# Attention units multiplied in float32 without splitting, and PSUM copies moved from ScalarE to VectorE

## What is computed

```python
q = jnp.einsum('bsh,oh->bso', x, Wq)   # 16 heads of 32, rotated
k = jnp.einsum('bsh,oh->bso', x, Wk)   # 4 heads of 32, rotated
v = jnp.einsum('bsh,oh->bso', x, Wv)
scores = jnp.einsum('bhqd,bhkd->bhqk', q, k) * scaling
attn = jax.nn.softmax(scores, axis=-1)
out = jnp.einsum('bhqk,bhkd->bhqd', attn, v)
...
x = x + 0.5 * ffn(layernorm(x))
x = x + attention(layernorm(x))
x = x + 0.5 * ffn(layernorm(x))
```

## Time and profile before

| | us |
|---|---|
| median of 3 runs | 1826.81 (1823.87 to 1834.07) |
| profiled execution, whole | 1813.59 |
| its span, first to last instruction | 1811.8 |
| first to last exponential of the attention stage | 661.6 to 1226.1 |
| PE busy | 1685.2 (93%) |
| DVE busy | 1081.7 (60%) |
| ACT busy | 857.9 (47%) |
| POOL busy | 977.0 (54%) |

### The profile page before, as it was taken

The page is one execution under the profiler, slowest core; times in us unless marked ns, Lnnn a source line. Parts: engine busy times, 40 slices in busy tenths (PEclk is TensorE's granted clock), DMA queues, the critical chain, the costliest instruction groups (busy, mean ns, idle before and its releaser), DMA issues.

```text
span 1811.8 us, 25089 instructions
## 1 busy us (share of the span) xinstructions
PE 1685.2 (93%) x8596; PEld 1342.8 (74%) x8596; DVE 1081.7 (60%) x1846; ACT 857.9 (47%) x1274; POOL 977.0 (54%) x727
## 2 busy tenths in 40 slices
PE   6999999999977989999999999887799999999997
PEld 5888899898866756666666666545688889999885
DVE  4554322222587879999999999995445432222226
ACT  4322232222224358989898988872333122322220
POOL 3115673336522148989898989840030619550646
PEclk9999999999988989999999999998989999999998
DMA  9205543333640000000000000003010535432427
GB/s 341 87 25 217 207 175 131 120 132 114 192 140 1 1 2 1 1 1 1 1 1 2 1 1 2 12 13 142 1 52 1 223 121 194 161 140 85 166 83 243
DMA packets 54310, 160.01 MB, mean 88 GB/s; under 512 B 6704, under 2 KB 7600, under 8 KB 51632
## 3 DMA queue, kind: packets, MB, share of 16 engines
q1 hardware_dynamic: 41360, 84.74, 13.4%
q0 software_dynamic: 12832, 73.67, 11.5%
HBM read 102.29 MB, written 55.84 MB: 87 GB/s over the span
## 4 chain that ended last, share of the span: by engine, by line
PE 58%; DVE 18%; issue 8%; ACT 7%; DMA 7%; POOL 0%; SPq 0%; ACTq 0%; DVEq 0%; POOLq 0%
PE PS L1050 10%; PE PS L1052 9%; PE PS L1051 9%; DVE nmf L1831 5%; DVE Ph L1848 4%; PE PS L1246 4%; DMA xn<-x_routed 3%; ACT Ph L1526 3%; ACT PT L1519 2%; DMA xs<-x_routed 2%; PE PS L1279 2%; PE PS L1172 2%; PE PS L1280 2%; PE PS L1177 2%; PE PS L1175 2%
## 5 line engine op out<-in xcount | busy, mean ns | idle before, releaser
L1988 POOL TENSOR_TENSOR Pl<-PT,Ph 128x1024 fp32r<-128x1024 f32 x176 | 435.9, 2491 | 81.6 <-ACT Ph L1526 76.4
L1831 DVE TENSOR_REDUCE nmf<-PS 128x1 f32<-128x1024 f32 x256 | 307.7, 1213 | 29.0 <-PE PS L1246 26.7
L1519 ACT ACTIVATE PT<-PS 128x1024 f32<-128x1024 f32 x256 | 258.7, 1015 | 19.9 <-DVE Pl L1854 11.7
L1279 PE MATMUL PS<-Ph,V 128*65 128x512 f32 x512 | 206.5, 403 | 11.9 <-DVE Pl L1854 10.9
L1280 PE MATMUL PS<-Pl,V 128*65 128x512 f32 x512 | 201.9, 394 | 0.0
L1526 ACT ACTIVATE Ph<-PT 128x1024 fp32r<-128x1024 f32 x184 | 194.1, 1055 | 1.5
L1903 POOL TENSOR_TENSOR W<-raw,W 128x544 fp32r<-128x544 f32 x144 | 190.1, 1354 | 1.5
L1806 DVE TENSOR_TENSOR thid<-thid,PS 128x352 f32<-128x352 f32 x78 | 40.6, 521 | 245.8 <-ACT thid L1445 245.8
L1246 PE MATMUL PS<-KS,QS 96*128 96x512 f32 x512 | 170.8, 415 | 16.9 <-ACT PT L1519 11.3
L1264 PE MATMUL PS<-QS,KS 98*128 98x512 f32 x512 | 174.8, 423 | 6.0 <-DVE nmf L1831 5.8
L1445 ACT ACTIVATE thid<-PS 128x352 f32<-128x352 f32 x78 | 36.2, 464 | 260.4 <-PE PS L1177 260.4
(11 more groups left out here) (183 smaller groups left out, 4111.9 us busy)
## 6 DMA issues: line engine op xcount, KB each, us to landing
raw<-ffn_w POOLq DMA_DIRECT2D x18, 2176.0 KB, 10.3
y_routed<-ytile SPq DMA_DIRECT2D x78, 256.0 KB, 2.0
xn<-x_routed SPq DMA_DIRECT2D x40, 256.0 KB, 2.9
x_routed<-xq SPq DMA_DIRECT2D x1, 9984.0 KB, 28.7
xs<-x_routed SPq DMA_DIRECT2D x38, 256.0 KB, 3.6
raw<-ffn_w SPq DMA_DIRECT2D x6, 768.0 KB, 10.4
raw<-ffn_w SPq DMA_DIRECT2D x2, 2176.0 KB, 9.1
x_home<-X SPq DMA_DIRECT2D x4, 1024.0 KB, 5.7
```

The source lines that it names most:

```text
L1279: e.matmul(PS[0:VCOL, ob, :], V[:, b * QT + kt, g, :], high_part(u)[:, js], start=kt == 0, stop=False)
L1519: e.activation(PT[:, u % PTBUF, :], PS[:, i:i + 2, :].rearrange("p b n -> p (b n)"), ACT.Exp, scale=SCALE).then_inc(p_ready.sem, 1)
L1831: e.tensor_reduce(nmf[:, (n % 3) * REP + h, t:t + 1], PS[:, i:i + 2, :].rearrange("p b n -> p (b n)"), AX.X, ALU.max, negate=True).then_in ...
L1988: e.tensor_tensor(low_part(u)[:], PT[:, u % PTBUF, :], high_part(u)[:], ALU.subtract).then_inc(pl_pool.sem, 1)
```

## The change

- `in_full` names units that aren't split: in group 7 the last pair of each half head (u % 4 = 3), in the groups before one unit in sixteen (u % 16 = 11, also a last pair). Their values are two float32 matmuls that read PT itself and V as float32, three units after the scores (FULL_LAG) and behind the unit's other work on PE. The last pair is then done before pair 2, so pair 2 ends the half head (`ends_half`).
- `hi_on_vector` is now true in group 7 alone, for pair 1; in groups 0 to 6 ACT takes all high parts. `lo_on_vector`: pair 1 in group 7; pair 2 before, but not the one ahead of a float32 unit (u % 16 = 10), whose low part goes to POOL.
- The copy of the output bank to OT moves from ACT to DVE in all groups; that of the query stack to QS moves from ACT to DVE in groups 0 to 5 (`beside_heads`).
- A PT buffer that a float32 unit used is free when its values are done, not when its low part is.
- At the end, the last unit's float32 matmuls come ahead of the values of the unit before it.

```diff
-LAG = 5
+LAG, FULL_LAG = 5, 3
...
+def in_full(u):
+
+    return u % 4 == 3 if in_last_group(u) else u % 16 == 11
+
+
+def in_last_group(u):
+    return u // UNITS == len(KV_GROUPS) - 1
+
+
 def hi_on_vector(u):
-    return u % 4 == 1 or u // UNITS == len(KV_GROUPS) - 1 and u % 4 == 3
+    return in_last_group(u) and u % 4 == 1
 
 
 def lo_on_vector(u):
-    return u % 4 == 2 or u // UNITS == len(KV_GROUPS) - 1 and u % 4 != 0
+    return u % 4 == 1 if in_last_group(u) else u % 4 == 2 and u % 16 != 10
+
+
+def ends_half(u):
+
+    return in_full(u + 1) if u % 4 == 2 else u % 4 == 3 and not in_full(u)
...
-        w = in_flight[0] if in_flight[0] == u - LAG else None
+        w = u - LAG if u >= LAG and not in_full(u - LAG) else None
...
+        if u >= FULL_LAG and in_full(u - FULL_LAG):
+            work.append(("values", u - FULL_LAG))
...
+    for w in [v for v in range(end - LAG, end - 2) if not in_full(v)] + [end - 1, end - 2]:
         work.append(("values", w))
...
-                e.matmul(PS[0:VCOL, ob, :], V[:, b * QT + kt, g, :], high_part(u)[:, js], start=kt == 0, stop=False)
-                mm = e.matmul(PS[0:VCOL, ob, :], V[:, b * QT + kt, g, :], low_part(u)[:, js],
-                              start=False, stop=kt == QT - 1)
+                end = ends_half(u) and j == 1
+                if in_full(u):
+                    mm = e.matmul(PS[0:VCOL, ob, :], V[:, b * QT + kt, g, :].bitcast(F32), PT[:, u % PTBUF, js],
+                                  start=False, stop=end)
+                else:
+                    e.matmul(PS[0:VCOL, ob, :], V[:, b * QT + kt, g, :], high_part(u)[:, js],
+                             start=kt == 0, stop=False)
+                    mm = e.matmul(PS[0:VCOL, ob, :], V[:, b * QT + kt, g, :], low_part(u)[:, js],
+                                  start=False, stop=end)
...
-            elif kind == "turn":
+            elif kind == "turn" and not beside_heads(key[0]):
...
-                if u >= PTBUF:
-                    act.wait_ge(pl_dve if lo_on_vector(u - PTBUF) else pl_pool, u - PTBUF)
+                if u >= PTBUF and in_full(u - PTBUF):
+                    act.wait_ge(pv_done, u - PTBUF)
+                elif u >= PTBUF:
+                    parts_ready(act, u - PTBUF)
...
-                e.activation(OT[0:VCOL, :], PS[0:VCOL, out_bank(n, hf), :], ACT.Copy).then_inc(ot_ready.sem, 1)
...
+            elif kind in VALUES and is_whole(key) and ends_half(key[0]):
...
+                dve.wait_ge(pv_done, u)
+                if i >= 1:
+                    dve.wait_ge(ot_turned, *heads[i - 1])
+                e.tensor_copy(OT[0:VCOL, :], PS[0:VCOL, out_bank(n, hf), :]).then_inc(ot_ready.sem, 1)
+            elif kind == "turn" and beside_heads(key[0]):
+                n, t = key
+                dve.wait_ge(stack_turned, n, t)
+                e.tensor_copy(QS[n % 3][0:STK, :, t * P:(t + 1) * P],
+                              PS[0:STK, MISC, :].rearrange("p (h n) -> p h n", n=P)).then_inc(stack_ready.sem, 1)
```

More of the change, by code:

```diff
@@ L396, in order_of_work @@
     work.append(("heads_start",))
-    in_flight, outputs, maxima, lows = [], [], [], []
+    outputs, maxima, lows = [], [], []
     groups = len(KV_GROUPS)
@@ L404, in order_of_work @@
             work.append(("spare_bank",))
[L405 to L408, removed]
+        in_parts = u > 0 and not in_full(u - 1)
+        if in_parts:
+            work.append(("split_hi", u - 1))
+            if not lo_on_vector(u - 1):
+                work.append(("split_lo", u - 1))
         work.append(("scores", u))
-        in_flight.append(u)
         if lows:
             work.append(("place_low", *lows.pop(0)))
-        w = in_flight[0] if in_flight[0] == u - LAG else None
+        w = u - LAG if u >= LAG and not in_full(u - LAG) else None
         between = w is not None and unit(w)[3] > 0 and n + 1 < groups
@@ L424, in order_of_work @@
             maxima.append((n + 1, un // QT))
-        if len(in_flight) > 1 and lo_on_vector(in_flight[-2]):
-            work.append(("split_lo", in_flight[-2]))
+        if in_parts and lo_on_vector(u - 1):
+            work.append(("split_lo", u - 1))
         if w is not None:
-            in_flight.pop(0)
             work.append(("half_values", w, 1) if between else ("values", w))
-            if unit(w)[3] == QT // 2 - 1:
+            if ends_half(w):
                 outputs.append(unit(w)[:3])
+        if u >= FULL_LAG and in_full(u - FULL_LAG):
+            work.append(("values", u - FULL_LAG))
         if outputs and pair == 1:
@@ L440, in order_of_work @@
             work.append(("wo", un // QT))
-    work.append(("split_hi", in_flight[-1]))
-    work.append(("split_lo", in_flight[-1]))
-    for w in in_flight:
+    end = groups * UNITS
+    assert in_full(end - 1) and LAG > FULL_LAG
+    for w in [v for v in range(end - LAG, end - 2) if not in_full(v)] + [end - 1, end - 2]:
         work.append(("values", w))
-        if unit(w)[3] == QT // 2 - 1:
-            outputs.append(unit(w)[:3])
-        elif outputs and unit(w)[3] == 1:
+        if outputs:
             work.append(("store_head", *outputs.pop(0)))
+    outputs.append(unit(end - 2)[:3])
     work.append(("store_head", *outputs.pop(0)))
@@ L840, in macaron @@
             pv_done.plan(u)
-            if unit(u)[3] == QT // 2 - 1:
+            if ends_half(u):
                 ot_ready.plan(*unit(u)[:3])
@@ L899, in is_projected_after, with parts_ready @@
         return PROJECTED.index(t) >= n
+    def parts_ready(lane, u):
+        if in_full(u):
+            lane.wait_ge(p_ready, u)
+        else:
+            lane.wait_ge(pl_dve if lo_on_vector(u) else pl_pool, u)
     def high_part(u):
@@ L921, in macaron @@
     ends = [tuple(unit(key[0])[:3]) for kind, *key in work
-            if kind in VALUES and is_whole(key) and unit(key[0])[3] == QT // 2 - 1]
+            if kind in VALUES and is_whole(key) and ends_half(key[0])]
     end_place = {key: i for i, key in enumerate(ends)}
@@ L1842, in vector_program @@
                     dve.wait_ge(home_out[g])
+            elif kind in VALUES and is_whole(key) and ends_half(key[0]):
+                u = key[0]
+                n, h, hf, pair = unit(u)
+                i = end_place[n, h, hf]
+                dve.wait_ge(pv_done, u)
[7 more added lines that the diff above has]
+                              PS[0:STK, MISC, :].rearrange("p (h n) -> p h n", n=P)).then_inc(stack_ready.sem, 1)
             elif kind == "split_hi" and hi_on_vector(*key):
```

6 lines of the change are left out of this document (4 added, 2 removed).

## The result

The changed kernel takes 1861.52 us (median of 4 runs, 1855.08 to 1868.77) against 1827.0 for the kernel before beside it: a ratio of 1.0185, 95% interval 1.0128 to 1.0241. It is slower by 34 us, where the forecast was 1827 and the range ended at 1850. Its profiled execution has a span of 1864.9 us.

The account below looks back on a forecast made before the run. No engine's busy time was taken to bound the attention stage, but waits between engines. The terms +11.4 - 1.6 - 8.8 - 1.1 = 0 us, set on the median 1826.8, gave 1827 us; range 1807 to 1850.

Parts of the forecast that it names:

- groups 0 to 5: Attention stage, twelve periods of sixteen units (four half heads): each goes from 35.95 to 36.9 us, +11.4 us in all.
- last group: Last attention group, first to last exponential: PE becomes the bound, 51.4 us, -12.2; holds give back 3.4, so -8.8 us.
- Second half head: Second of a period's four half heads, groups 0 to 5: 8.48 us, with PE waiting 0.2 for the output copy.
- Rival 1: Attention stage: PE alone sets the pace, copies on DVE never late; period 33.8, 45 us faster, 1782; chance 0.12.
- Third: Third half head of a period, groups 0 to 5, no low part on DVE, maxima transposed: 8.46 us.
- First: First half head of a period (units 0 to 3), groups 0 to 5, DVE coming late after a float32 unit: 8.42 us.
- Fourth: Fourth half head of a period, groups 0 to 5, with the float32 matmuls in front of its last unit: 11.05 us.
- The 0.5 for a held low part: Added once per period in groups 0 to 5 for a DVE low part held by POOL's; estimate between 0 and 2.2.
- rival 4: PE's float32 matmuls: their passes don't overlap, 3.1 us a unit; +31 us, 1858; chance 0.07.
- rival 2: Attention stage: no holds occur and the float32 unit takes three passes; some 18 us faster, 1809; chance 0.11.
- The last group's holds: Last group: DVE's parts held behind POOL's low parts, output copy behind these; four times 0.85, 3.4 us lost.
- Rival 3: Attention groups: DVE's low part loses to POOL's and is held 2.2 us once a period; +20 us, 1847; chance 0.25.

## Why the prediction was wrong

| term of the sum | predicted | measured |
|---|---|---|
| groups 0 to 5 | +11.4 | +33.1 |
| group 6 | -1.6 | +4.4 |
| last group | -8.8 | -4.2 |
| tail behind the last exponential | -1.1 | -1.2 |
| sum | 0 | +32 |

(Measured: 1134.1 - 670.2 = 463.9 against 1092.4 - 661.6 = 430.8; then the stretches above against the earlier trace rows.)

**The step that failed** is the line of the Second half head, "maximum and output copy 1.84, PE's store 0.05 + 0.31, a unit 1.86": it lets PE run on to the store before it needs DVE's copy, and so finds a wait of 0.2. PE needs it one half unit sooner, 0.93, because the next half head's first values go into the same bank. The code shows it, `until_free(ob)` at pair 0, and the prediction used it for nothing. Rival 1's working has the same error, "PE asks for the copy at 2 x 1.86 = 3.7": the values ask at 2.8. With the deadline 0.93 earlier the wait is 0.2 + 0.93 = 1.13; the trace shows 1.16. The half head becomes 8.48 + 0.93, and 0.11 more because the copy reaches PE 0.82 after its start (874.09 to 874.91) and not 0.71: 9.52. Measured from low part to low part, 871.23 to 880.76, it is 9.53. From exponential to exponential the Third is 9.64, predicted 8.46, with the same wait of 1.16 (at 884.45); the First came out at 8.95 against 8.42, the Fourth at 10.69 against 11.05, and these two differences were not taken apart. The 0.5 for a held low part did not occur. Together, 1.05 + 1.18 + 0.53 - 0.36 - 0.5 = 1.9, the step from 36.9 to 38.80. Group 6 has the same single bank and the same error.

**Right** were the prices: the copy 0.60 to DVE's next (0.58), the low part 1.13 (872.36 - 871.23), the tail 5.71 against 5.75 (1268.01 to the end of the last row here). The float32 unit, in PE's timeline of the changed kernel with what follows it,

```profile
896.60 1.88 PE L1302 MATMUL PS<-PT,V 128*65 128x512 f32 x4
897.92 1.03 PE L1285 MATMUL PS<-QS,KS 98*128 98x512 f32 x2
898.79 0.39 PE L1305 MATMUL PS<-Ph,V 128*65 128x512 f32 x1
...
1273.32 0.40 PE L1307 MATMUL PS<-Pl,V 128*65 128x512 f32 x1
```

takes 898.79 - 896.60 less 0.46 for the scores, 1.73, where 1.74 was taken: rival 4 did not occur, and of rival 2 only the missing holds, in groups 0 to 6. (Its sum is a little off: 0.85 x 12, 3.4, 2.5 and 1 make 17 us, not 18.) Right too were PE's small wait for the store's last step, and DVE's idle time while a unit runs:

```profile
861.12 1.23 DVE L1852 TENSOR_REDUCE nmf<-PS 128x1 f32<-128x1024 f32 x1 [2.35 <-PE PS L1267]
```

**The last group's holds** were mis-sized: -8.8 held 3.4 for them, and 4.6 more was lost. (The 63.61 before had a granted clock of 0.97; what that cost there is not shown.) Casts are held as well as low parts, one behind the other, and the output copy comes behind them (DVE, then GpSimd, then PE, changed kernel):

```profile
1227.54 2.63 DVE L1882 CAST Ph<-PT 128x1024 fp32r<-128x1024 f32 x1
1230.21 3.31 DVE L1888 TENSOR_TENSOR Pl<-PT,Ph 128x1024 fp32r<-128x1024 f32 x1
1233.44 0.68 DVE L1871 COPY OT<-PS 65x512 f32<-65x512 f32 x1
```

```profile
1227.25 5.18 POOL L2022 TENSOR_TENSOR Pl<-PT,Ph 128x1024 fp32r<-128x1024 f32 x2
```

```profile
1234.17 0.46 PE L1317 MATMUL PS<-identf,OT 65*128 65x65 f32 x4 [1.19 <-DVE OT L1871]
```

Three runs without float32 units in groups 0 to 6, at full clock throughout, show what this cost: with the output copy on VectorE, with it on ScalarE, and with GpSimd's low parts moved to VectorE besides (the last group, columns as above):

```profile
1201.99:1261.42 59.43, 53.54 (x224) 30.20 (x223) 46.09 (x58) 47.65 (x49) 50.27 (x25) 1.00 0.04 14
1141.32:1197.26 55.94, 53.08 (x224) 30.37 (x223) 40.92 (x49) 50.46 (x58) 54.80 (x24) 1.00 0.04 15
1139.26:1194.17 54.91, 52.64 (x224) 30.52 (x223) 41.36 (x65) 50.35 (x58) 12.24 (x9) 1.00 0.05 15
```

So the output copy behind the held parts cost 3.5, and GpSimd's low parts, once no output copy stood behind DVE's, only 1.0. No run came to the 51.4 that the prediction gave PE alone.

**Of the rivals**, rival 1 was right in its direction once the output copy was out of the way (a period of 35.24 with the float32 units, 34.05 without them, against its 33.8), and wrong for the changed kernel. Rival 3 gave nearly the right time (1847 and more) for a wrong reason: in groups 0 to 6 of the changed kernel DVE's low parts were never held (42 of them, 1.21 to 1.22 us). That the race can be lost is shown by the copy moved ahead of the maximum. The list of what would prove the forecast wrong did not hold the row that did: PE's values waiting for OT.

## What to carry to other kernels

A copy that frees a buffer is due when the buffer's next writer wants it, not when the copy's reader does; before moving one to another engine, look for every wait on it, and count from the earliest. An engine with 20% idle time can still be late at that place, in every round, because its queue is served in order: moving one 0.6 us copy ahead of a 1.1 us maximum was worth 3.4 us in 38 without the float32 units (with them it cost 1.5, by lost races). And a change of several parts should be priced part by part, in the surroundings in which it will run: with the output copy on ScalarE the stack copy on VectorE gave 1.1 a period and the casts on ScalarE 1.65, while with the output copy on VectorE the same stack copy cost 1.35. The output copy and, in each pair of runs, the float32 units outside the last group were losses. What the last group's float32 units are worth was not tested.

## What was not expected of the hardware

A cast on VectorE, with one input, is held by GpSimd's low part as a subtraction with two is: 2.63 us in the changed kernel and 2.10 with the output copy on ScalarE, where it takes 0.68 to 0.70 when not held. The Trainium skill (SBUF — State Buffer, Who interferes with whom) names casts among what can contend; the rows agree.

A start 0.12 us earlier or 0.39 later decides between 1.22 and 3.10 us for VectorE's subtraction, and nothing in the program's order shows which it will be: the same list of instructions on DVE ran with either from one period to the next.
